# Rounding constants of FP4 codes: from Exp of the absolute value on ScalarE, in place of a clipped square from ScalarE and VectorE

## The reference

```python
# block 1: a state space layer, 16 states n per channel, scanned along the length l
u  = silu(conv3(x))
B, C = split(u @ W_bc + b_bc)
dt = softplus((u @ W_dt + b_dt) @ W_dtp + b_dtp)
h[l, n] = exp(-exp(A_log[n]) * dt[l]) * h[l-1, n] + B[l, n] * x[l] * dt[l]
x = layernorm(x + (sum_n C[l, n] * h[l, n] + x * Dcoeff))
# block 2: a gated FFN (128 -> 352 -> 128) whose activations and weights go through FP4
def fp4(v):                              # in blocks of 16 along the last dimension
    scale = max(|block|) / 6
    xn = v / scale
    return GRID[searchsorted(MID, |xn|)] * sign(xn) * scale
    # GRID 0, .5, 1, 1.5, 2, 3, 4, 6;  MID .25, .75, 1.25, 1.75, 2.5, 3.5, 5
x = layernorm(x + fp4(silu(fp4(x) @ fp4(w_gate).T) * (fp4(x) @ fp4(w_up).T)) @ fp4(w_down).T)
```

## Time and profile before

| | |
|---|---|
| time, median of 3 runs | 358.61 us (358.43 to 363.51) |
| the profiled execution | 362.16 us, span 360.4 us |
| busy: VectorE, GpSimd, PE, ScalarE | 320.5, 282.1, 262.3, 229.8 us |
| TensorE's granted clock, mean | 0.927 of full |

### The profile page before, as it was taken

The page is one execution under the profiler, slowest core; times in us unless marked ns, Lnnn a source line. Parts: engine busy times, 40 slices in busy tenths (PEclk is TensorE's granted clock), DMA queues, the critical chain, the costliest instruction groups (busy, mean ns, idle before and its releaser), DMA issues.

```text
span 360.4 us, 4013 instructions
## 1 busy us (share of the span) xinstructions
PE 262.3 (73%) x1130; PEld 122.3 (34%) x1130; DVE 320.5 (89%) x366; ACT 229.8 (64%) x505; POOL 282.1 (78%) x170
## 2 busy tenths in 40 slices
PE   2675849697847778777877889688977682877672
PEld 1222312222321235323442345133523450336372
DVE  3869978899999999999999999999999999857860
ACT  3475834865587558974798569856985476245444
POOL 0095556579378999999999999899989999943762
PEclk9969985879998999999999999999989789598999
DMA  3760650083007400560048003900290001000002
GB/s 50 157 153 2 139 123 2 0 183 79 0 2 156 109 1 2 131 160 0 3 106 186 0 2 81 210 1 4 53 209 2 0 0 30 0 4 0 29 2 58
DMA packets 19262, 21.86 MB, mean 61 GB/s; under 512 B 6112, under 2 KB 15144, under 8 KB 19240
## 3 DMA queue, kind: packets, MB, share of 16 engines
q1 hardware_dynamic: 18520, 21.05, 25.9%
q10 hardware_dynamic: 720, 0.56, 0.8%
HBM read 2.72 MB, written 2.10 MB: 13 GB/s over the span
## 4 chain that ended last, share of the span: by engine, by line
POOL 24%; PE 21%; ACT 16%; DVE 14%; issue 12%; SPq 8%; DMA 3%; DVEq 0%; ACTq 0%; POOLq 0%
POOL product L825 10%; SPq L479 7%; DVE states L1101 5%; PE ps_prep L1410 4%; DVE db L1081 3%; POOL qh_norm L846 3%; POOL qh_norm L841 3%; PE ps_y L1388 3%; ACT ps_decay L528 3%; ACT r_feat L614 2%; DMA dt_rep<-dtx 2%; POOL rstd L835 2%; POOL qx_norm L846 2%; POOL qx_norm L841 2%; ACT hq_t L662 2%
## 5 line engine op out<-in xcount | busy, mean ns | idle before, releaser
L825 POOL TENSOR_TENSOR product<-states,c_rep 128x1024 f32<-128x1024 f32 x58 | 136.7, 2364 | 27.3 <-DVE states L1101 27.2
L528 ACT ACTIVATE ps_decay<-dt_rep,aneg 128x512 f32<-128x512 f32 x128 | 87.1, 690 | 45.7 <-DVE states L1101 40.1
L1081 DVE SCALAR_TENSOR_TENSOR db<-ps_b,bbc_rep,dt_rep 128x2048 f32<-128x2048 f32 x31 | 72.5, 2338 | 3.7 <-DMA dt_rep<-dtx 3.5
L1101 DVE TENSOR_TENSOR_SCAN states<-ps_decay,db 128x512 f32<-128x512 f32 x64 | 75.3, 1202 | 0.2
L1101 DVE TENSOR_TENSOR_SCAN states<-ps_decay,states,db 128x512 f32<-128x512 f32 x52 | 64.3, 1261 | 0.2
L1430 PE MATMUL ps_b<-u_feat,wbc_rep 128*128 128x512 f32 x64 | 39.5, 702 | 19.3 <-DVE db L1081 19.2
L1423 PE MATMUL ps_prep<-u_feat,wbc_rep 128*128 128x512 f32 x56 | 32.0, 655 | 16.7 <-ACT c_rep L606 16.6
L1388 PE MATMUL ps_y<-product,gather 128*32 128x512 f32 x248 | 35.7, 654 | 2.8 <-POOL product L825 2.6
L1459 PE MATMUL ps_f<-gate_t,xq_t 128*128 128x352 f32 x48 | 20.6, 511 | 12.4 <-DVE hidden L1151 8.2
L1410 PE MATMUL ps_prep<-x_feat,tap_diag 128*128 128x512 f32 x42 | 22.4, 644 | 4.5 <-issue 4.5
L633 ACT ACTIVATE gate_tanh<-ps_f 128x352 f32<-128x352 f32 x26 | 12.0, 463 | 20.5 <-PE ps_f L1459 18.7
(11 more groups left out here) (245 smaller groups left out, 539.1 us busy)
## 6 DMA issues: line engine op xcount, KB each, us to landing
dt_rep<-dtx SPq DMA_DIRECT2D x124, 128.0 KB, 2.4
x_tok<-in_L_attn_x SPq DMA_DIRECT2D x8, 256.0 KB, 3.3
out<-y_out SPq DMA_DIRECT2D x7, 256.0 KB, 2.5
dt_rep<-dtx ACTq DMA_DIRECT2D x4, 128.0 KB, 3.7
out<-y_out SPq DMA_DIRECT2D x2, 128.0 KB, 2.0
hidden<-in_L_ffn_w_down SPq DMA_DIRECT2D x1, 176.0 KB, 3.6
x_feat<-in_L_attn_x SPq DMA_DIRECT2D x8, 0.5 KB, 2.9
hidden<-in_L_ffn_w_gate SPq DMA_DIRECT2D x1, 128.0 KB, 2.9
```

Source lines behind the costliest of these rows:

```text
L528: nc.scalar.activation(ps_decay[BANK_OF[k]][:], dt_rep[p][:, c, 0, :], ACT.Exp, scale=aneg[:, c, m:m + 1]).then_inc(decay_done, 1)
L825: nc.gpsimd.tensor_tensor(product[:, j % PRODUCTS], groups(s, 2 * j, 2), over(c_rep[p][:, j // SET_PAIRS, :], 2), ALU.mult).then_inc(produ ...
L1081: nc.vector.scalar_tensor_tensor(out=db[m % DB][:], in0=over(ps_b[:], QUADS), scalar=bbc_rep[:, 0, m:m + 1], in1=dt_rep[p][:, :, 1, :], op ...
L1101: nc.vector.tensor_tensor_scan(out=groups(s, k, 1)[:, 0, :], data0=ps_decay[BANK_OF[k]][:], data1=db[k // QUADS % DB][:, k % QUADS, :], in ...
```

## The change

`magic` becomes `exp(rate * |norm| + start)` in bf16, with rate and start such that the result has the same power of two as before over each range of the grid. ScalarE makes it in two steps, Abs and Exp. VectorE's clip goes from the steps; the head's and the tail's FP4 stay as they were (square and clip).

- `x`, slot 9 of ScalarE: Square becomes Abs (`x_size`, dense) and Exp, the second waiting for the first.
- `h`: Square at slot 8 goes; Abs at slot 10 and Exp at slot 11, in place in `qh_magic`.
- VectorE: L1041 goes from slots 9 and 10. GpSimd waits for the same semaphores, which ScalarE now raises.
- `y_out` goes from slot 11 to slot 12 of ScalarE.
- A constant `step_start` (128x1) is set at VectorE's start.

```diff
@@ constants
+STEP_START = math.log(1.03125 * 2.0 ** 22)
+STEP_RATE = math.log(2.0 / 1.03125) / 2.05
@@ AT
-    "act variance": 8, "act y": 11, "act x square": 9, "act h square": 8,
+    "act variance": 8, "act y": 12, "act x steps": 9, "act h size": 10, "act h steps": 11,
...
-    "dve x quant": {0: (7, False), 1: (7, False), 2: (8, True), 5: (10, False)},
-    "dve h quant": {0: (3, False), 1: (3, False), 2: (4, False), 5: (9, False)},
+    "dve x quant": {0: (7, False), 1: (7, False), 2: (8, True)},
+    "dve h quant": {0: (3, False), 1: (3, False), 2: (4, False)},
@@ ScalarE
+            def steps(size, magic):
+
+                return nc.scalar.activation(magic, size, ACT.Exp, scale=STEP_RATE, bias=step_start[:])
+
+            def steps_of_x(f):
                 act.wait_ge(x_norm_done, f.at(1, 1))
                 if f.beyond(1):
                     act.wait_ge(x_magic_done, f.at(1))
+                nc.scalar.activation(x_size, qx.norm[:], ACT.Abs).then_inc(x_size_done, 1)
+                act.wait_ge(x_size_done, f.at(1, 1))
+                steps(x_size, qx.magic[:, 0:TILES * D]).then_inc(x_magic_done, 1)
+
+            def size_of_h(g):
+                act.wait_ge(h_norm_done, g.at(1, 1))
+                nc.scalar.activation(qh.magic[:], qh.norm[:], ACT.Abs).then_inc(h_size_done, 1)
+
+            def steps_of_h(g):
+                act.wait_ge(h_size_done, g.at(1, 1))
+                steps(qh.magic[:], qh.magic[:]).then_inc(h_magic_done, 1)
...
-                    if f is not None and k == AT["act x square"]:
-                        square_x(f, qx.norm)
-                    if g is not None and k == AT["act h square"]:
-                        square_h(g)
+                    if f is not None and k == AT["act x steps"]:
+                        steps_of_x(f)
+                    if g is not None and k == AT["act h size"]:
+                        size_of_h(g)
+                    if g is not None and k == AT["act h steps"]:
+                        steps_of_h(g)
@@ VectorE, quantization of x (that of h loses the same)
-                    elif n == 5:
-                        dve.wait_ge(x_square_done, f.at(1, 1))
-                        if f.beyond(1):
-                            dve.wait_ge(xq_done, f.at(1))
...
-                    last = quant_op(9 if n == 5 else n, src, None, qx, TILES * D)
+                    last = quant_op(n, src, None, qx, TILES * D)
```

More of the change, by code:

```diff
@@ L21 @@
+import math
 import concourse.bass as bass
@@ L210, in build @@
         eps = sb("eps", [128, TILES])
+        step_start = sb("step_start", [128, 1])
         center = sb("center", [128, 128])
@@ L268, in build @@
         x_square = sb("x_square", [128, TILES * D // BLOCK + 1, BLOCK + 2], bf16)
+        x_size = x_square[:].rearrange("p b k -> p (b k)")[:, 0:TILES * D]
         def flat(t):
@@ L393, in build @@
         h_magic_done = sem("h_magic_done")
+        x_size_done = sem("x_size_done")
+        h_size_done = sem("h_size_done")
         h_code_order = sem("h_code_order")
@@ L518, in _ @@
                 act.dma_start(alog[:, c, :], channels[c].broadcast_to([STATES, E, N])).then_inc(alog_in, 16)
-            act.wait_ge(setup_order, 1)
+            act.wait_ge(setup_order, 2)
             nc.scalar.activation(table_in[:, 0:1], x_feat[0][:, 0:1], ACT.Exp)
@@ L643, in x1_of @@
                 last.then_inc(x1_done, 1)
-            def square_x(f, norm):
+            def steps(size, magic):
+                return nc.scalar.activation(magic, size, ACT.Exp, scale=STEP_RATE, bias=step_start[:])
+            def steps_of_x(f):
                 act.wait_ge(x_norm_done, f.at(1, 1))
@@ L648, in square_x @@
                     act.wait_ge(x_magic_done, f.at(1))
+                nc.scalar.activation(x_size, qx.norm[:], ACT.Abs).then_inc(x_size_done, 1)
[7 more added lines that the diff above has]
+                steps(qh.magic[:], qh.magic[:]).then_inc(h_magic_done, 1)
+            def square_x(f, norm):
+                act.wait_ge(x_norm_done, f.at(1, 1))
+                act.wait_ge(x_magic_done, f.at(1))
                 nc.scalar.activation(x_square[:, 0:TILES * D // BLOCK, 0:BLOCK], blocked(norm[:]), ACT.Square,
@@ L960, in _ @@
             setup.unit(Unit(0))
+            setup.mark(nc.vector.memset(step_start[:], STEP_START))
             setup.mark(nc.vector.memset(x_feat[0][:, 0:1], 0.0))
@@ L1130, in gate @@
                             dve.wait_ge(xq_done, f.at(1))
-                    elif n == 5:
-                        dve.wait_ge(x_square_done, f.at(1, 1))
-                        if f.beyond(1):
-                            dve.wait_ge(xq_done, f.at(1))
                     else:
                         order_g.need()
-                    last = quant_op(9 if n == 5 else n, src, None, qx, TILES * D)
+                    last = quant_op(n, src, None, qx, TILES * D)
                     if n == 2:
                         last.then_inc(x_inv_done, 1)
-                    elif n == 5:
-                        last.then_inc(x_magic_done, 1)
                         assert order_g.n == DVE_GATE, order_g.n
@@ L1165, in quant @@
                             dve.wait_ge(hq_done, g.at(1))
-                    elif n == 5:
-                        dve.wait_ge(h_square_done, g.at(1, 1))
                     else:
                         order_q.need()
-                    last = quant_op(9 if n == 5 else n, flat(hidden[:]), None, qh, TILES * INNER, HIDDEN_SCALE)
+                    last = quant_op(n, flat(hidden[:]), None, qh, TILES * INNER, HIDDEN_SCALE)
                     if n == 2:
                         last.then_inc(h_inv_done, 1)
-                    elif n == 5:
-                        last.then_inc(h_magic_done, 1)
                         assert order_q.n == DVE_QUANT, order_q.n
@@ L1246, in codes_of_x @@
                 def codes_of_x(src):
-                    dve.wait_ge(x_square_done, f.at(1, 1))
+                    dve.wait_ge(x_square_done, 1)
                     quant_op(9, src, None, qx, TILES * D).then_inc(x_magic_done, 1)
@@ L1310, in tail @@
                 codes_of_x(src)
-                quant(g, *AT["dve h quant"][5])
+                dve.wait_ge(h_square_done, 1)
+                quant_op(9, None, None, qh, TILES * INNER, HIDDEN_SCALE).then_inc(h_magic_done, 1)
                 dve.wait_ge(h_magic_done, g.at(1, 1))
```

## The result

| | before | changed |
|---|---|---|
| first comparison: median of the executions | 359.63 us (358.43 to 363.51) | 369.76 us (365.50 to 370.37) |
| ratio to before, 95% interval | | 1.0245 [1.0147, 1.0344] |
| measured again, with more executions | 361.41 us | 367.08 us, ratio 1.0142 [1.0094, 1.0190] |
| the profiled execution; its span | 362.16; 360.4 us | 365.50; 363.7 us |

The forecast was 356.8 us and the range ended at 360.0. Both intervals lie above 1: the kernel got slower. A ratio compares executions of either kernel that lie within 1.5% of that kernel's fastest. The profiled execution is the fastest of the five, so its trace shows less than the whole loss.

What follows compares the result with a forecast made beforehand. The 16 `dt_rep` transfers with VectorE's work were taken to set the 37.23 us step. Gains of 0.4 + 0.3 us in steady steps and 0.8 + 0.3 at the end, 1.8 us, gave 358.61 - 1.8 = 356.8 us; range 353.8 to 360.0.

Steps and rivals of the forecast that it cites:

- is ScalarE late anywhere?: Count of ScalarE's work from the decays' end to `xq_t` and first tanh: 11.4 us, about 0.9 us kept in hand.
- It costs nothing: Moving y one slot later delays SyncE's store by 2 to 3 us, harmless while the `dt_rep` transfers queue ahead of it.
- The first rival: ScalarE becomes late before `xq_t` and first tanh, VectorE waits at `hidden`: up to 362.8 us; chance 0.15.
- decides from 0.9 us of lateness: At VectorE's `hidden`: ScalarE's lateness beyond the count costs time from 0.9 us, each further us one us in five steps.
- the sum: 0.4 + 0.3 us in the steady steps, 0.8 + 0.3 at the end: 1.8 us off the median 358.61.
- The prices: ScalarE's Abs and Exp: 0.63 and 0.69 us for x, 1.36 and 1.45 for h; 2.1 us more a step.
- VectorE's wait for the transfers: At `db` of slot 14, VectorE's wait for `dt_rep` grows from 0.25 us or nothing to about 0.7 us a step.
- the variance wait: GpSimd's 0.79 us idle for ScalarE's variance of h goes; steady steps replace it by scan waits, the end keeps the gain.
- the norm of x in the last step: On GpSimd it takes 1.35 us beside a VectorE clip, 1.05 us in the steady step; 0.3 us gained.
- The gain: Whole kernel 1.8 us faster, 356.8 us, about half from steady steps and the rest from the end; counted as no change.
- The third rival: Steady steps stay as they are and the 1.1 us at the end are lost in the tail: 358.3 us; chance 0.10.
- The base loop: `dtx` to `db` over 16 transfers, 12.35 us, plus VectorE's work to the next `dtx`, 24.88 us: gives the step's 37.23 us.

Runs made afterwards that it cites:

- the unread matmuls: Changed kernel plus four TensorE matmuls a step that nobody reads: 364.14 us, ratio 1.0068; the kernel before with the same four: 362.68 us, 1.0004.

## Why the prediction was wrong

- **The step that failed** is the question "is ScalarE late anywhere?". It followed ScalarE's own list to `xq_t` and to the first tanh, and both came where it said: `xq_t` 15.1 us behind `dtx` (said 15.0), the first tanh at 16.6 (said 16.6 to 17.0), and VectorE didn't wait for it. That agreement is luck: ScalarE was through its own list at 14.0 us, a microsecond earlier than counted, and then stood 1.07 us for TensorE's transposes, a wait that the count put at nothing. ScalarE also feeds TensorE on the way. The `c_rep` of slot 12, behind Exp of h and y, releases the C product, and TensorE has transposes, two products, a B product and eight sums to do between it and the gate product of tile 1. That list had 0.52 us of slack at this product, and the way from it to VectorE's `hidden` 0.7 to 1.0 us in all; ScalarE took 1.28 to 1.65 us. Swapping `c_rep` and y gave all of it back (1.0020).
- **"It costs nothing"** for y one slot later: true of y alone (1.0006), and even with Exp of h (0.9986), but the reason given was SyncE's queue. It fails together with both pairs, and then y at slot 11 is no better: what matters is that `y_out` stands ahead of `c_rep`. The same holds for x alone and h alone. I priced each edit against the slack as it stood before, and they share it.
- **The first rival** had the right end (VectorE waits at `hidden`) and the wrong road, and "decides from 0.9 us of lateness" was read at tile 0; at tile 1 it was 0.52 us of TensorE's idle time. Its price, 362.8 us, was too low as well, as was its chance of 0.15.
- **The clock** was missing from the sum. The earlier trace rows gives 1.00 for the steady step of before, and I took it as given. By the unread matmuls it makes up an estimated 3 of the change's 6 us, but only as the order has made TensorE's list late.
- **The prices** were right: Abs and Exp of x 0.64 and 0.72 us, of h 1.36 and 1.46, no table load between them. (The row of 0.597 us in the earlier trace rows, read as Identity without a bias, is a tanh; the price came out right even so.) VectorE's wait for the transfers grew as said (0.41 to 0.86 us), the variance wait went, and the norm of x in the last step fell from 1.35 us to 1.06.
- **The gain** of 1.8 us was not found in any kernel with the whole change: with ScalarE in time it measures 1.0020 and 0.9981, no change. Its make-up was off too. 1.2 of the 1.8 us were to come from the variance, and 0.6 from the clips; but the kernel without clips keeps the variance's place and its wait, and gains 2.5 us. That this is near 1.8 is luck. The third rival's 358.3 us doesn't follow from its words either: steps as they are and nothing at the end give 358.6.
- **The base loop** was half right. `dtx` to `db` takes 12.3 us, by the issues, and in one step of four opening it gave 1.2 us. But GpSimd, busy for 36.1 of the step's 37.2 us, with its wait of 0.79 us fills all but 0.3 us of the step as well, and in the other three steps it stays when the loop over the transfers is opened. Two loops of one length can't be told apart in a trace; taking one away does it.

The Trainium skill (ScalarE: Activation LUTs, Rules for kernel authors) wants a max or min on VectorE. By the runs its advice holds here for the outcome, but not through the price of the instruction: with the same dear instructions in another place the time is that of before.

## What to carry to other kernels

Follow a lengthened engine's list to each instruction that another engine waits for, not only to the one that you think of as its last, and read at every such place who waited for whom before: the waits in the other direction along that way, here 0.7 to 1.0 us, are all the slack there is. Price edits to one engine together, since each may be free and the sum not. When two neighbours in a list feed different engines, put first the one with the longer list behind it.

## What the runs showed of the hardware

- The issue of a transfer on SyncE took 0.63 us whether it carried 128 KB or 64 KB (16 of them 10.04 and 10.19 us).
- Reading bf16 made Exp no cheaper on ScalarE: 0.72 us for 512 elements with a bias, where the decays' Exp of 512 fp32 elements took 0.67 to 0.71 us; 1408 elements took 1.46 us, against 1.36 us for Abs reading fp32.
- The granted clock of TensorE fell to 1.2 GHz for stretches of some microseconds, also in kernels as fast as before; a pair of 512-column matmuls then took 1.96 instead of 1.12 us. A wait of TensorE of 2.06 us had either level behind it, and with h alone waits of 2.07 to 2.46 us in every step left the clock at 1.00. In these profiles a stretch cost time where TensorE's list was the one waited for (steps of 39.0 to 40.5 us), and none where it wasn't (36.73 us with and without).
